# Rounding steps of the activation quantization: which engine runs them, in a two-layer kernel on eight cores

## The chip, the cores and the metric

The kernel runs on one Trainium2 chip, on all 8 of its cores. Each core computes one of the 8 sequences of the batch; the cores exchange nothing. The time is the device time in microseconds of the slowest core. A core has TensorE (PE, matrix products into eight PSUM banks), VectorE (DVE), ScalarE (ACT), GpSimd (POOL), SyncE (SP) and 16 DMA engines. The engines run their own instruction streams in the order in which they were written and meet at semaphores only.

## The reference

Input x is [8, 2048, 1024]. Two layers, each attention then feed-forward, and after each of the four the residual sum is layer-normalized:

- layer 0 attention is a time-mixed linear recurrence (four 1024x1024 products), layer 0 feed-forward has a gated pair of 1024 to 4096 products, two 4096x4096 products and one back to 1024;
- layer 1 attention is gated linear attention with 4 heads. Each of its products (q, k, v, g, gk1, gk2, o) takes a quantized input;
- layer 1 feed-forward is 1024 to 4096, a depthwise convolution over 3 tokens, silu, 4096 to 1024, both products with quantized inputs.

The quantization, which is all that the change touches, is

```
def act_quant(x):
    scale = 127.0 / jnp.clip(jnp.max(jnp.abs(x), axis=-1, keepdims=True), 1e-05)
    return jnp.clip(jnp.round(x * scale), -128.0, 127.0) / scale
```

with one scale for each token (the last axis is the features).

## The kernel before

The residual stream stays in SBUF as `XA`, feature-major. `Prog` records the instructions of each engine in the order in which the stage functions emit them; nothing reorders them. `P.op(engine, fn, after=[...])` appends one instruction and returns a token; `after` lists the tokens waited for. `vt` carries the last VectorE token through a stage, `stt` the last ScalarE token.

**Rounding.** `_round_fix` (L1398) rounds 128x1024 values in `Zb`: a cast to int32 into `Ib` (L1399), a cast back to bf16 into `Tb` (L1400), the difference `Zb - Tb` into `Db` (L1401), and two compare-and-add steps (L1404, L1406) which correct the cast whichever way it rounds. Every caller passes `en = "v"`, so all of it runs on VectorE; the branch for another engine is never taken.

**Its four callers**, and how often each calls it:

- `stage_l1attn`, projections: 8 blocks of 256 tokens, 5 projections (q, k, v, g, gk1, in this order), 2 groups of 128 tokens (`tt`): 80 calls. A call begins with the product with the norm weights (L991), the maximum (L995), four small steps (L998 to L1006), and the scaling by a column (L1010); after the rounding come the rescaling (L1013), eight transposes on TensorE (L1023) and two copies into `XQF` (L1029). After both groups the projection's matmuls follow (L1067 for q and k, L1086 for v and g, L1044 for gk1). The results leave PSUM on VectorE for q, k, v and gk1, and for g on ScalarE with silu (L1101): eight of those a block.
- `stage_l1attn`, the output product: per block 2 chunks of 128 tokens and 2 halves: 32 calls, with a scaling L1331 ahead and L1334 behind.
- `stage_l1ffn`, input: 4 quarters of 512 tokens, 4 groups: 16 calls, with L1540 ahead and L1543 behind.
- `_act_quant_fm` (L1421), the 4096 hidden features of a quarter: 16 pieces of 1024 columns in each of 4 quarters: 64 calls. Each is preceded by a product of two tensors (L1427) and followed by L1432 and L1434. The product waits for the end of the piece before it (`ch = vt`).

The weights of the projections come through one buffer `WL`, filled by POOL's queue; the norm weights through one buffer `NB`.

Of the kernel before, what the change touches and what calls it, by code (L numbers as in the profile page):

```python
# [10 lines left out]
AF = mybir.ActivationFunctionType  # L11
ALU = mybir.AluOpType
# [871 lines left out]
def stage_l1attn(ctx, toks):  # L884
# [6 lines left out]
    with ExitStack() as st_:  # L891
# [48 lines left out]
        vt = vz2  # L940
# [13 lines left out]
        for blk_i in range(8):  # L954
# [27 lines left out]
            for pi, (pnm, wnm, nnm, dout) in enumerate(NPROJ):  # L982
# [3 lines left out]
                for tt in range(2):  # L986
                    en = "v"
                    Zb, Ib, Tb, Db = (QSz, QSi, QSt, QSd) if tt == 0 else (Q2z, Q2i, Q2t, Q2d)
                    CLx = CL if tt == 0 else CL2
                    ch = vt  # L990
                    p1 = P.op(en, lambda v, tt=tt, Zb=Zb: v.tensor_mul(  # L991
                        Zb[:], X2[:, tt, :], NB[:, 0:1024]),
                        after=[d_nb, x2tok, ch, zb_free[tt]])
                    nb_free2[tt] = p1
                    p2 = P.op("v", lambda v, Zb=Zb, CLx=CLx: v.reduce_max(  # L995
                        CLx[:, 4:5], Zb[:], axis=AXX, apply_absolute_value=True),
                        after=[p1, vt])
# [12 lines left out]
                    q1 = P.op(en, lambda v, Zb=Zb, CLx=CLx: v.tensor_single_scalar(  # L1010
                        Zb[:], Zb[:], CLx[:, 7:8], ALU.mult), after=[p6, ch])
                    q6 = _round_fix(P, en, Zb, Ib, Tb, Db, Zb, q1)
                    q7 = P.op(en, lambda v, Zb=Zb, Tb=Tb, CLx=CLx: v.tensor_scalar(  # L1013
                        Zb[:], Tb[:], 1.0, CLx[:, 8:9], ALU.subtract, ALU.mult),
                        after=[q6])
                    vt = q7
                    xtp = []
                    for c in range(NC):
                        bank = 5 + c // 4
                        cc = c % 4  # L1020
                        a = [q7, bank_free[bank]] if (c % 4 == 0) else []
                        xtp.append(P.op("t", lambda t, c=c, bank=bank, cc=cc, Zb=Zb:
                                        t.transpose(  # L1023
                            PSB[bank][:, cc * 128:(cc + 1) * 128],
                            Zb[:, c * 128:(c + 1) * 128], IDB[:]), after=a))
                    zb_free[tt] = xtp[-1]
                    for half in range(2):
                        bank = 5 + half
                        ev = P.op("v", lambda v, tt=tt, half=half, bank=bank: v.tensor_copy(  # L1029
                            XQF[:, half * 4:(half + 1) * 4, tt * 128:(tt + 1) * 128],  # L1030
                            PSB[bank][:, 0:512].rearrange("p (c n) -> p c n", c=4)),
                            after=[xtp[half * 4 + 3], vt])
                        vt = ev
                        bank_free[bank] = ev
                    qtoks.append(vt)
# [151 lines left out]
            for cn in range(2):  # L1187
# [135 lines left out]
                for half in range(2):  # L1323
# [4 lines left out]
                        Zb[:], OG[:, half * 1024:(half + 1) * 1024],  # L1328
                        NOB[:, half * 1024:(half + 1) * 1024]),
                        after=[ch, w7, zb_free[half]])  # L1330
                    y2 = P.op(en, lambda v, Zb=Zb: v.tensor_single_scalar(  # L1331
                        Zb[:], Zb[:], CL[:, 7:8], ALU.mult), after=[y1])
                    y7_ = _round_fix(P, en, Zb, Ib, Tb, Db, Zb, y2)
                    y8 = P.op(en, lambda v, Zb=Zb, Tb=Tb: v.tensor_scalar(  # L1334
                        Zb[:], Tb[:], 1.0, CL[:, 8:9], ALU.subtract, ALU.mult),
                        after=[y7_])
# [58 lines left out]

def _round_fix(P, en, Zb, Ib, Tb, Db, M, prev):  # L1398
# [4 lines left out]
    if en == "v":
        o4 = P.op(en, lambda v, Tb=Tb, Db=Db: v.scalar_tensor_tensor(  # L1404
            Tb[:], Db[:], 0.5, Tb[:], ALU.is_ge, ALU.add), after=[o3])
        o5 = P.op(en, lambda v, Tb=Tb, Db=Db: v.scalar_tensor_tensor(  # L1406
            Tb[:], Db[:], -0.5, Tb[:], ALU.is_gt, ALU.add), after=[o4])
    else:
        o4a = P.op(en, lambda v, Db=Db, M=M: v.tensor_single_scalar(
            M[:], Db[:], 0.5, ALU.is_ge), after=[o3])  # L1410
        o4 = P.op(en, lambda v, Tb=Tb, M=M: v.tensor_add(Tb[:], Tb[:], M[:]),
                  after=[o4a])
        o5a = P.op(en, lambda v, Db=Db, M=M: v.tensor_single_scalar(
            M[:], Db[:], -0.5, ALU.is_gt), after=[o4])
        o5 = P.op(en, lambda v, Tb=Tb, M=M: v.tensor_add(Tb[:], Tb[:], M[:]),
                  after=[o5a])
    return o5


def _act_quant_fm(P, flat, UB, WB, QSV, QSG, vt, gt, ready=None):  # L1420
    piece = 1024  # L1421
    for pc in range(16384 // piece):
        o0 = pc * piece
# [3 lines left out]
        q1 = P.op(en, lambda v, o0=o0: v.tensor_mul(  # L1427
            flat[:, o0:o0 + piece], flat[:, o0:o0 + piece], UB[:, 0:piece]),
            after=[ch, ready if pc < 2 else None])
        q6 = _round_fix(P, en, flat[:, o0:o0 + piece], QI[:, 0:piece],  # L1430
                        QT[:, 0:piece], QD[:, 0:piece], QM[:, 0:piece], q1)
        q7 = P.op(en, lambda v, QT=QT: v.tensor_scalar(  # L1432
            QT[:, 0:piece], QT[:, 0:piece], 1.0, None, ALU.subtract), after=[q6])
        q8 = P.op(en, lambda v, o0=o0, QT=QT: v.tensor_mul(  # L1434
            flat[:, o0:o0 + piece], QT[:, 0:piece], WB[:, 0:piece]), after=[q7])
        vt = q8
    return vt, gt


def stage_l1ffn(ctx, toks):  # L1440
# [5 lines left out]
    with ExitStack() as st_:  # L1446
# [51 lines left out]
        for q in range(4):  # L1498
# [7 lines left out]
            for tt in range(4):  # L1506
# [5 lines left out]
                for c in range(NC):  # L1512
# [121 lines left out]
            for which, COLS, ROW in ((0, MX[:, 0:4], UR), (1, MX[:, 4:8], WR)):  # L1634
                for tt in range(4):
# [180 lines left out]
```

How the kernel before makes its waits and increments, by code:

```python
            def body(eng):  # L145
                seen = {}
                for i, rec in enumerate(prog.ops[e]):
                    for kind, val in rec["waits"]:
                        if seen.get(kind, 0) >= val:
                            continue
                        eng.wait_ge(prog.sems[kind], val)
                        seen[kind] = val
                    inst = rec["fn"](eng)
                    if rec["dma"] is not None:
                        inst.then_inc(prog.sems[rec["dma"]], 16)
                    amt = incs[e].get(i)
                    if amt:
                        inst.then_inc(prog.sems[e], amt)
```

## Time and profile before

| | |
|---|---|
| median of 3 runs | 12169.72 us (12141.12 to 12209.28) |
| the profiled execution's own time | 12209.73 us |
| its span on the slowest core (core 3), first to last instruction | 12208.2 us |
| spans of the eight cores | 12118.2 to 12208.2 us |
| mean granted TensorE clock, cores 0 to 3 and 4 to 7 | 0.697 and 0.704 |
| layer 1 attention, from the span's start | 6360 to 9880 us |
| layer 1 feed-forward | 10034 to 12110 us |

The profile is of one execution, on its slowest core. "Busy" counts an engine's instructions, not its waits, and a share over the whole span mixes eight stages with different limits; so the two stages that quantize are to be read by themselves. In a timeline a row gives the start, the duration, the engine, the line and the operation, and in brackets how long the engine had been idle and what released it. The granted clock is a share of 2.4 GHz; 0.5 is the lower of TensorE's two levels, 1.2 GHz.

### The profile page before, as it was taken

The page shows a single profiled execution, that of the slowest core. Times are in us where ns is not written, and L with a number is a line of the kernel's source. Part 1 is how long each engine was busy: PE and PEld are TensorE (multiplying, and loading weights), DVE is VectorE, ACT ScalarE, POOL GpSimd, SP SyncE. Part 2 cuts the span into 40 slices and gives each one's busy share as a digit, 9 for nine tenths or more (in the row PEclk, how much of TensorE's full clock was granted, in tenths as well). Part 3 has the DMA queues.
Part 4 walks back from the last instruction along what each step waited for, and adds up shares of the span by engine and source line. Part 5 has one row for each costly group of instructions (what it writes and reads, how often), then busy time and mean ns, then how long its engine had stood idle before and what let it go on. Part 6 is the DMA issues. An engine that isn't in the chain of part 4 may idle for free.

```text
span 12208.2 us, 72294 instructions; the slowest of 8 cores (12118.2 to 12208.2 us)
## 1 busy us (share of the span) xinstructions
PE 5413.1 (44%) x22678; PEld 2575.2 (21%) x22678; DVE 3719.3 (30%) x6428; ACT 1286.9 (11%) x2046; POOL 780.4 (6%) x1515
## 2 busy tenths in 40 slices
PE   3430016666666666666643333333333332413323
PEld 1120002222222222222221222222122221101112
DVE  6762231000000100000024444444444435353553
ACT  1232100000000100000021001001001021001011
POOL 0000450000000000000000000000000000000000
PEclk7765557888878787878766666666666666756666
DMA  4224432222222222222211111111111101101012
GB/s 114 76 73 125 139 92 40 43 42 45 45 38 43 39 43 42 42 42 43 41 29 52 60 44 43 60 52 40 55 60 43 54 14 30 55 11 45 25 30 78
DMA packets 171208, 637.27 MB, mean 52 GB/s; under 512 B 30976, under 2 KB 31360, under 8 KB 159568
## 3 DMA queue, kind: packets, MB, share of 16 engines
q0 software_dynamic: 125696, 480.99, 16.2%
q1 hardware_dynamic: 45136, 151.67, 4.2%
q8 instruction: 187, 3.06, 0.1%
q14 instruction: 189, 1.55, 0.0%
HBM read 794.50 MB, written 42.01 MB: 69 GB/s over the span
## 4 chain that ended last, share of the span: by engine, by line
PE 40%; DVE 27%; DMA 19%; issue 8%; ACT 4%; DVEq 1%; POOL 1%; ACTq 0%; SPq 0%; POOLq 0%
PE ps L824 17%; PE ps L776 5%; DMA f_wj<-h1R 4%; DMA f_wj<-h2R 4%; PE ps L1672 2%; PE ps L861 2%; DMA f_wj<-w1R 2%; PE ps L1086 2%; PE ps L1253 2%; PE ps L1571 1%; PE ps L1371 1%; DMA pre_in<-f1T 1%; DMA pre_in<-f2T 1%; PE ps L1067 1%; DMA b_wj<-q_f2T 1%
## 5 line engine op out<-in xcount | busy, mean ns | idle before, releaser
L824 PE MATMUL ps<-f_h,f_wj 128*128 128x512 bf16 x8192 | 2080.1, 422 | 1106.0 <-DMA f_wj<-h1R 554.8
L824 PEld LDWEIGHTS ps<-f_h,f_wj 128*128 128x128 bf16 x8192 | 868.6, 106 | 2317.5 <-issue 1648.6
L872 DVE SCALAR_TENSOR_TENSOR XA<-ps,SVEC,XA 128x512 f32<-128x512 f32 x32 | 24.0, 751 | 3547.3 <-PE ps L861 3544.9
L776 PE MATMUL ps<-f_h,f_wj 128*128 128x512 bf16 x2048 | 576.9, 452 | 527.5 <-DMA f_wj<-w1R 520.6
L1672 PE MATMUL ps<-b_hc,b_wj 128*128 128x512 bf16 x1024 | 281.3, 443 | 611.7 <-DVE b_hc L1434 469.3
L835 ACT ACTIVATE f_h<-ps,f_sc 128x512 bf16<-128x512 f32 x256 | 176.5, 689 | 2960.6 <-PE ps L824 2948.4
L776 PEld LDWEIGHTS ps<-f_h,f_wj 128*128 128x128 bf16 x2048 | 229.7, 112 | 874.3 <-issue 720.3
L1086 PE MATMUL ps<-a_wl,a_xqf 128*128 128x512 bf16 x1024 | 305.2, 471 | 150.7 <-DMA a_wl<-q_gwT 68.8
L796 DVE SCALAR_TENSOR_TENSOR f_h<-ps,f_sc,f_g 128x512 bf16<-128x512 f32 x128 | 96.1, 751 | 781.9 <-ACT f_g L786 775.2
L861 PE MATMUL ps<-f_h,f_wj 128*128 128x512 bf16 x1024 | 251.4, 411 | 137.3 <-DMA f_wj<-w3R 137.3
L1233 PE MATMUL ps<-a_qg,a_kp 128*128 128x128 f32 x256 | 76.4, 454 | 523.5 <-DVE a_kg L1226 523.5
L1616 PE MATMUL ps<-c_idb,b_hc 128*128 128x128 bf16 x512 | 74.9, 302 | 524.0 <-ACT b_hc L1599 397.6
L1672 PEld LDWEIGHTS ps<-b_hc,b_wj 128*128 128x128 bf16 x1024 | 111.1, 111 | 786.3 <-issue 705.0
L536 PE MATMUL ps<-l_xk,l_wk 128*128 128x512 bf16 x256 | 105.6, 587 | 351.9 <-DVE l_xr L522 190.3
L408 PE MATMUL ps<-pre_acc,c_ones 128*128 128x1 f32 x18 | 4.5, 319 | 570.0 <-POOL pre_acc L401 570.0
L1571 PE MATMUL ps<-b_xq,b_wj 128*128 128x512 bf16 x1024 | 238.9, 387 | 19.5 <-DMA b_wj<-q_f1T 11.7
L1371 PE MATMUL ps<-a_oqf,a_wl 128*128 128x128 bf16 x2048 | 177.1, 270 | 146.8 <-DMA a_wl<-q_owT 133.2
L694 PE MATMUL ps<-c_idf,ln_tm 128*128 128x128 f32 x384 | 93.2, 424 | 310.0 <-DVE ln_tm L675 310.0
L1023 PE MATMUL ps<-c_idb,a_q2z 128*128 128x128 bf16 x320 | 40.4, 306 | 417.5 <-DVE a_q2z L1013 417.5
L431 DVE TENSOR_SCALAR pre_in<-pre_in,pre_rs 128x1024 f32<-128x1024 f32 (+1 forms) x137 | 100.2, 732 | 395.4 <-DMA pre_in<-f1T 129.5
L1575 ACT ACTIVATE b_h<-ps,SCL 128x512 bf16<-128x512 f32 x128 | 88.3, 690 | 1248.0 <-PE ps L1571 1248.0
L1253 PE MATMUL ps<-a_S,a_qg 128*128 128x512 f32 x256 | 218.3, 1004 | 0.0
(338 smaller groups left out, 7677.3 us busy)
## 6 DMA issues: line engine op xcount, KB each, us to landing
f_wj<-h1R POOLq DMA_DIRECT2D x128, 512.0 KB, 5.9
f_wj<-h2R POOLq DMA_DIRECT2D x128, 512.0 KB, 5.7
a_wl<-q_owT POOLq DMA_DIRECT2D x32, 2048.0 KB, 7.7
b_wj<-q_f2T POOLq DMA_DIRECT2D x80, 512.0 KB, 4.7
pre_in<-f1T SPq DMA_DIRECT2D x64, 512.0 KB, 4.1
pre_in<-f2T SPq DMA_DIRECT2D x64, 512.0 KB, 3.9
a_wl<-q_vwT POOLq DMA_DIRECT2D x16, 2048.0 KB, 7.6
a_wl<-q_gwT POOLq DMA_DIRECT2D x16, 2048.0 KB, 7.6
```

What stands on the lines that cost most here:

```text
L431: v1 = P.op("v", lambda v: v.tensor_single_scalar(buf[0:rr, 0:cc], buf[0:rr, 0:cc], pre["rs"][0:rr, :], ALU.mult), after=[ld, state["v"]])
L536: mmK = P.op("t", lambda t, c=c, i=i, bk=bk: t.matmul(PS[bk][:, :], WK[:, i, c * 128:(c + 1) * 128], XK[:, i, :], start=(i == 0), stop=(i ...
L776: t.matmul(PS[bank][:, :], wb[:, i, :], XB[:, i, s2 * 512:(s2 + 1) * 512], start=(i == 0), stop=(i == NC - 1)),
L824: off=off, SRC=SRC: t.matmul(PS[bank][:, :], wb[:, i2, :], SRC[:, i * 1024 + off:i * 1024 + off + 512], start=(i == 0), stop=(i == 31)),
L835: DST=DST: s.activation(DST[:, j * 1024 + off:j * 1024 + off + 512], PS[bank][:, :], AF.Gelu, scale=SC[:, scoff + j:scoff + j + 1]),
L861: off=off: t.matmul(PS[bank][:, :], wb[:, i2, :], H0[:, i * 1024 + off:i * 1024 + off + 512], start=(i == 0), stop=(i == 31)),
L1067: mm = P.op("t", lambda t, i=i, j=j, bank=bank: t.matmul(PS[bank][:, 0:256], WLv[:, i, j * 128:(j + 1) * 128], XQF[:, i, :], start=(i == 0 ...
L1086: t.matmul(PS[bank][:, :], XQF[:, i, tt * 128:(tt + 1) * 128], WLv[:, i, ds * 512:(ds + 1) * 512], start=(i == 0), stop=(i == NC - 1)),
L1253: omm = P.op("t", lambda t, h=h, j=j: t.matmul(PS[3][:, :], QG[:, j, :], S[:, 2 * h + j, :], start=(j == 0), stop=False), after=[f3, bank_ ...
L1371: cc=cc: t.matmul(PS[bank][:, cc * 128:(cc + 1) * 128], WLv[:, i, jj * 128:(jj + 1) * 128], OQF[:, rnd * 8 + i, :], start=(rnd == 0 and i ...
L1571: mm = P.op("t", lambda t, slot=slot, i=i, j=j, bank=bank: t.matmul(PS[bank][:, :], FWJ[slot][:, i, :], XQ3[:, i, :], start=(i == 0), stop ...
L1672: t.matmul(PS[bank][:, :], FWJ[s_][:, i2, :], HC[:, i, :], start=(i == 0), stop=(i == 31)),
```

## The change

The two casts of `_round_fix` are now ScalarE activations with the function Identity. The difference and the two corrections stay on VectorE. In three of the four callers the scaling just ahead of the rounding goes to ScalarE too, as an Identity with a column as its scale; in `_act_quant_fm` the product ahead of it stays on VectorE. The ScalarE token is threaded through (`stt`). The unused branch and the argument's effect are gone.

```
@@ stage_l1attn, projections (stage_l1attn output and stage_l1ffn input alike)
-                    q1 = P.op(en, lambda v, Zb=Zb, CLx=CLx: v.tensor_single_scalar(
-                        Zb[:], Zb[:], CLx[:, 7:8], ALU.mult), after=[p6, ch])
-                    q6 = _round_fix(P, en, Zb, Ib, Tb, Db, Zb, q1)
+                    q1 = P.op("s", lambda s, Zb=Zb, CLx=CLx: s.activation(
+                        Zb[:], Zb[:], AF.Identity, scale=CLx[:, 7:8]),
+                        after=[p6, ch, stt])
+                    stt = q1
+                    q6, s6 = _round_fix(P, en, Zb, Ib, Tb, Db, Zb, q1, stt)
+                    stt = s6
...
@@ _round_fix
-    o1 = P.op(en, lambda v, Zb=Zb, Ib=Ib: v.tensor_copy(Ib[:], Zb[:]), after=[prev])
-    o2 = P.op(en, lambda v, Ib=Ib, Tb=Tb: v.tensor_copy(Tb[:], Ib[:]), after=[o1])
-    o3 = P.op(en, lambda v, Zb=Zb, Tb=Tb, Db=Db: v.tensor_sub(Db[:], Zb[:], Tb[:]),
-              after=[o2])
...
+    o1 = P.op("s", lambda s, Zb=Zb, Ib=Ib: s.activation(Ib[:], Zb[:], AF.Identity),
+              after=[prev, sprev])
+    o2 = P.op("s", lambda s, Ib=Ib, Tb=Tb: s.activation(Tb[:], Ib[:], AF.Identity),
+              after=[o1])
+    o3 = P.op("v", lambda v, Zb=Zb, Tb=Tb, Db=Db: v.tensor_sub(Db[:], Zb[:], Tb[:]),
+              after=[o2, prev])
...
+    return o5, o2
@@ _act_quant_fm
-        q6 = _round_fix(P, en, flat[:, o0:o0 + piece], QI[:, 0:piece],
-                        QT[:, 0:piece], QD[:, 0:piece], QM[:, 0:piece], q1)
+        q6, s6 = _round_fix(P, en, flat[:, o0:o0 + piece], QI[:, 0:piece],
+                            QT[:, 0:piece], QD[:, 0:piece], QM[:, 0:piece], q1, st[0])
+        st[0] = s6
```

On VectorE, the quantization of the first group for gk1 in the first block stands in a row like this before (`a_q...` are the quantization's buffers, `a_cl` its columns, `a_xqf` the transposed result, `a_x` the input in token-major form):

```order
L998 TENSOR_SCALAR a_cl<-a_cl 128x1
L1001 RECIPROCAL a_cl<-a_cl 128x1
L1003 SCALAR_TENSOR_TENSOR a_cl<-a_cl 128x1
L1006 TENSOR_SCALAR a_cl<-a_cl 128x1
L1010 TENSOR_SCALAR a_qz<-a_qz,a_cl 128x1024
L1399 CAST a_qi<-a_qz 128x1024
L1400 CAST a_qt<-a_qi 128x1024
L1401 TENSOR_TENSOR a_qd<-a_qz,a_qt 128x1024
L1404 SCALAR_TENSOR_TENSOR a_qt<-a_qd,a_qt 128x1024
```

Of the changed kernel the same place reads, the difference's line being L1409 now:

```order
L998 TENSOR_SCALAR a_cl<-a_cl 128x1
L1001 RECIPROCAL a_cl<-a_cl 128x1
L1003 SCALAR_TENSOR_TENSOR a_cl<-a_cl 128x1
L1006 TENSOR_SCALAR a_cl<-a_cl 128x1
L1409 TENSOR_TENSOR a_qd<-a_qz,a_qt 128x1024
L1411 SCALAR_TENSOR_TENSOR a_qt<-a_qd,a_qt 128x1024
L1413 SCALAR_TENSOR_TENSOR a_qt<-a_qd,a_qt 128x1024
```

Three instructions of 128x1024 are gone from VectorE's row, and nothing has come in between: L1006 is followed by the difference that needs their result.

On ScalarE, in the first block of the attention, the row before is this (`a_sg` is the gate, `a_wf` and `a_g1t` belong to the decay; x8 are the eight silu of g):

```order
L978 ACTIVATE a_cl<-a_cl 128x2
L1101 ACTIVATE a_sg<-ps,SCL 128x512 x8
L1109 ACTIVATE a_wf,a_cl<-a_g1t 128x16
L1118 ACTIVATE a_cl<-a_cl 128x1
L1109 ACTIVATE a_wf,a_cl<-a_g1t 128x16
```

In the changed kernel it is this, from the second group's quantization for g on (L1104 is the silu's line there, L1112 the decay's):

```order
L1010 ACTIVATE a_q2z<-a_q2z,a_cl 128x1024
L1405 ACTIVATE a_q2i<-a_q2z 128x1024
L1407 ACTIVATE a_q2t<-a_q2i 128x1024
L1104 ACTIVATE a_sg<-ps,SCL 128x512 x8
L1010 ACTIVATE a_qz<-a_qz,a_cl 128x1024
L1405 ACTIVATE a_qi<-a_qz 128x1024
L1407 ACTIVATE a_qt<-a_qi 128x1024
L1010 ACTIVATE a_q2z<-a_q2z,a_cl 128x1024
L1405 ACTIVATE a_q2i<-a_q2z 128x1024
L1407 ACTIVATE a_q2t<-a_q2i 128x1024
L1112 ACTIVATE a_wf,a_cl<-a_g1t 128x16
```

The three steps of gk1's first group now stand behind all eight silu of g on the same engine. In all, VectorE has 512 instructions fewer and ScalarE 512 more (3 x 128 + 2 x 64); the rows of POOL and SP are the same as before.

## Rows read from the trace of the kernel before

**Rows 1.** Section 1 of the page: busy us, share of span, instructions.
```profile
PE 5413.1 (44%) x22678; PEld 2575.2 (21%) x22678; DVE 3719.3 (30%) x6428; ACT 1286.9 (11%) x2046; POOL 780.4 (6%) x1515
```

**Rows 2.** Attention and feed-forward stretch: length, busy PE, PEld, DVE, ACT, POOL, then clock.
```profile
6360.00:9880.00 3520.00, 1300.28 (x6360) 766.78 (x6360) 1640.86 (x3155) 323.78 (x548) 66.01 (x124) 0.64 0.15 51
10034.00:12110.00 2076.00, 678.28 (x3134) 303.20 (x3132) 959.61 (x1542) 183.47 (x261) 110.60 (x208) 0.64 0.12 37
```

**Rows 3.** Section 4 of the page: the chain that ended last, by engine.
```profile
PE 40%; DVE 27%; DMA 19%; issue 8%; ACT 4%; DVEq 1%; POOL 1%; ACTq 0%; SPq 0%; POOLq 0%
```

**Rows 4.** Timeline, quantization before the k projection: start, us, engine, line, operation.
```profile
6855.23 0.15 DVE L1006 TENSOR_SCALAR a_cl<-a_cl 128x1 f32<-128x1 f32 x1
6855.49 0.49 DVE L1010 TENSOR_SCALAR a_q2z<-a_q2z,a_cl 128x1024 bf16<-128x1024 bf16 x1
6856.08 0.69 DVE L1399 CAST a_q2i<-a_q2z 128x1024 int32<-128x1024 bf16 x1
6856.88 0.69 DVE L1400 CAST a_q2t<-a_q2i 128x1024 bf16<-128x1024 int32 x1
6857.68 0.69 DVE L1401 TENSOR_TENSOR a_q2d<-a_q2z,a_q2t 128x1024 bf16<-128x1024 bf16 x1
...
6861.77 1.01 PE L1023 MATMUL ps<-c_idb,a_q2z 128*128 128x128 bf16 x8 [10.32 <-DVE a_q2z L1013]
```

**Rows 5.** Groups of ScalarE instructions, shapes apart: busy us, mean ns, idle before.
```profile
L1101 ACT ACTIVATE a_sg<-ps,SCL 128x512 bf16<-128x512 f32 x64 | 44.1, 689 | 143.3 <-PE ps L1086 143.2
...
L1204 ACT ACTIVATE a_et<-a_gt 128x256 f32<-128x256 f32 x64 | 26.8, 418 | 6.2 <-ACT a_qg L1201 0.4
...
L560 ACT ACTIVATE l_sr<-ps 128x512 bf16<-128x512 f32 x32 | 19.1, 598 | 0.4
...
L1282 ACT ACTIVATE a_wf<-a_og 128x1024 f32<-128x1024 bf16 x16 | 16.9, 1058 | 156.1 <-DVE a_og L1274 156.1
...
L672 ACT ACT_TABLE_LOAD x3 | 3.8, 1283 | 4.4 <-DVE ln_cols L670 4.4
```

**Rows 6.** Timeline: hand-overs between VectorE and ScalarE, and on ScalarE alone.
```profile
7018.75 1.91 ACT L1181 ACTIVATE a_wf<-a_wf 128x2048 f32<-128x2048 f32 x1 [0.37 <-ACT a_wf L1179]
...
7029.92 0.48 DVE L1218 TENSOR_SCALAR a_et<-a_gt 128x128 f32<-128x128 f32 x2
7030.55 0.42 ACT L1222 ACTIVATE a_et<-a_et 128x256 f32<-128x256 f32 x1 [1.73 <-DVE a_et L1218]
7031.07 0.43 DVE L1226 TENSOR_TENSOR a_kg<-a_et,a_k 128x256 f32<-128x256 f32 x1 [0.67 <-ACT a_et L1222]
...
7079.46 1.06 ACT L1282 ACTIVATE a_wf<-a_og 128x1024 f32<-128x1024 bf16 x1 [9.13 <-DVE a_og L1274]
7080.43 0.19 ACT L1282 ACTIVATION_READ_ACCUMULATOR a_wf<-a_og 128x1 f32 x1
```

**Rows 7.** Timeline, quantization before gk1, first 128 tokens: blocks 1, 2 and 8.
```profile
6536.83 0.69 DVE L1401 TENSOR_TENSOR a_qd<-a_qz,a_qt 128x1024 bf16<-128x1024 bf16 x1
...
6539.60 0.69 ACT L1101 ACTIVATE a_sg<-ps,SCL 128x512 bf16<-128x512 f32 x1 [1.04 <-PE ps L1086]
...
6973.57 0.69 DVE L1401 TENSOR_TENSOR a_qd<-a_qz,a_qt 128x1024 bf16<-128x1024 bf16 x1
...
6976.42 0.69 ACT L1101 ACTIVATE a_sg<-ps,SCL 128x512 bf16<-128x512 f32 x1 [1.04 <-PE ps L1086]
...
6977.03 0.59 DVE L1013 TENSOR_SCALAR a_qz<-a_qt,a_cl 128x1024 bf16<-128x1024 bf16 x1
...
9609.39 0.69 DVE L1401 TENSOR_TENSOR a_qd<-a_qz,a_qt 128x1024 bf16<-128x1024 bf16 x1
...
9611.88 0.69 ACT L1101 ACTIVATE a_sg<-ps,SCL 128x512 bf16<-128x512 f32 x1 [1.04 <-PE ps L1086]
```

**Rows 8.** Timeline, one piece of the feature-major quantization.
```profile
10319.58 0.69 DVE L1427 TENSOR_TENSOR b_hc<-b_hc,b_ub 128x1024 bf16<-128x1024 bf16 x1
...
10321.97 0.69 DVE L1401 TENSOR_TENSOR b_qd<-b_hc,b_qt 128x1024 bf16<-128x1024 bf16 x1
```

More of the change, by code:

```diff
@@ L1330, in stage_l1attn @@
                         after=[ch, w7, zb_free[half]])
-                    y2 = P.op(en, lambda v, Zb=Zb: v.tensor_single_scalar(
-                        Zb[:], Zb[:], CL[:, 7:8], ALU.mult), after=[y1])
-                    y7_ = _round_fix(P, en, Zb, Ib, Tb, Db, Zb, y2)
+                    y2 = P.op("s", lambda s, Zb=Zb: s.activation(
+                        Zb[:], Zb[:], AF.Identity, scale=CL[:, 7:8]),
+                        after=[y1, stt])
+                    stt = y2
+                    y7_, sy = _round_fix(P, en, Zb, Ib, Tb, Db, Zb, y2, stt)
+                    stt = sy
                     y8 = P.op(en, lambda v, Zb=Zb, Tb=Tb: v.tensor_scalar(
@@ L1394, in stage_l1attn, with _round_fix, _act_quant_fm @@
         return dict(v=P.tok("v"), t=P.tok("t"), s=P.tok("s"))
-def _round_fix(P, en, Zb, Ib, Tb, Db, M, prev):
-    o1 = P.op(en, lambda v, Zb=Zb, Ib=Ib: v.tensor_copy(Ib[:], Zb[:]), after=[prev])
-    o2 = P.op(en, lambda v, Ib=Ib, Tb=Tb: v.tensor_copy(Tb[:], Ib[:]), after=[o1])
-    o3 = P.op(en, lambda v, Zb=Zb, Tb=Tb, Db=Db: v.tensor_sub(Db[:], Zb[:], Tb[:]),
-              after=[o2])
[L1403 to L1420, printed above, removed]
+def _round_fix(P, en, Zb, Ib, Tb, Db, M, prev, sprev=None):
+    o1 = P.op("s", lambda s, Zb=Zb, Ib=Ib: s.activation(Ib[:], Zb[:], AF.Identity),
[4 more added lines that the diff above has]
+              after=[o2, prev])
+    o4 = P.op("v", lambda v, Tb=Tb, Db=Db: v.scalar_tensor_tensor(
+        Tb[:], Db[:], 0.5, Tb[:], ALU.is_ge, ALU.add), after=[o3])
+    o5 = P.op("v", lambda v, Tb=Tb, Db=Db: v.scalar_tensor_tensor(
+        Tb[:], Db[:], -0.5, Tb[:], ALU.is_gt, ALU.add), after=[o4])
+    return o5, o2
+def _act_quant_fm(P, flat, UB, WB, QSV, QSG, vt, gt, ready=None, stt=None):
+    st = [stt]
     piece = 1024
@@ L1436, in _act_quant_fm @@
         vt = q8
-    return vt, gt
+    return vt, gt, st[0]
 def stage_l1ffn(ctx, toks):
@@ L1539, in stage_l1ffn @@
                 vt = a5
-                b1 = P.op(en, lambda v, Zb=Zb, CLx=CLx: v.tensor_single_scalar(
-                    Zb[:], Zb[:], CLx[:, 3:4], ALU.mult), after=[a5, ch])
-                b6 = _round_fix(P, en, Zb, Ib, Tb, Db, MSKF[tt % 2], b1)
+                b1 = P.op("s", lambda s, Zb=Zb, CLx=CLx: s.activation(
+                    Zb[:], Zb[:], AF.Identity, scale=CLx[:, 3:4]),
+                    after=[a5, ch, stt])
+                stt = b1
+                b6, sb6 = _round_fix(P, en, Zb, Ib, Tb, Db, MSKF[tt % 2], b1, stt)
+                stt = sb6
                 b7 = P.op(en, lambda v, Zb=Zb, Tb=Tb, CLx=CLx: v.tensor_scalar(
@@ L1654, in stage_l1ffn @@
                 bank_free[6] = bev
-            vt, gt = _act_quant_fm(P, HC[:, :, :].rearrange("p c n -> p (c n)"),
-                                   UB, WB, (QI, QT, QD, MSKF[0]),
-                                   (Q2i, Q2t, Q2d, MSKF[1]), vt, gt, ready=vt)
+            vt, gt, stt = _act_quant_fm(P, HC[:, :, :].rearrange("p c n -> p (c n)"),
+                                        UB, WB, (QI, QT, QD, MSKF[0]),
+                                        (Q2i, Q2t, Q2d, MSKF[1]), vt, gt,
+                                        ready=vt, stt=stt)
             hq_tok = (vt, gt)
```

## The prediction

> **What bounds the kernel now.** I read the page's busy shares first, then the busy time of the two stages that quantize, the chain of waits, and last the timeline of single calls. The shares [rows 1] show no full engine: TensorE 44%, VectorE 30%, ScalarE 11%. The two stages alone [rows 2] say more: in the attention's 3520 us VectorE is busy for 1641 (47%) and ScalarE for 324 (9%), in the feed-forward's 2076 us it is 960 (46%) and 183 (9%). ScalarE looks like free room. But a share can't say whether an engine is waited for. The chain [rows 3] gives VectorE 27% of the span, nearly its whole busy share. The timeline shows why [rows 4]: from the last column step (L1006) to the difference (L1401) VectorE runs L1010, L1399 and L1400 with gaps of 0.1 us, and TensorE's transposes end an idle of 10.32 us on this chain. One call is one string of dependent steps; nobody else works meanwhile. So what counts is not VectorE's load but how long the string is from L1006's end to L1401's start.
>
> **What the string costs now.** L1006 ends at 6855.38 and L1401 starts at 6857.68 [rows 4]: 2.30 us for 0.49 + 0.69 + 0.69 and four gaps. In the feature-major pieces only the two casts lie in it: L1427 ends at 10320.27, L1401 starts at 10321.97 [rows 8]: 1.70 us.
>
> **What it costs on ScalarE.** No row of before shows an activation from bf16 to int32 or back.
>
> - An activation of 128x1024 from bf16 takes 1058 ns (L1282), which I take for each cast [rows 5]. Underneath I bound it by VectorE's own 0.69 [rows 4].
> - The scaling has a column as its scale. At 128x512 from PSUM one with a scale column (L1101) takes 689 ns and one without (L560) 598 [rows 5], so a column costs 91; 1058 + 91 = 1149 ns.
> - VectorE to ScalarE: L1218 ends at 7030.40, L1222 starts at 7030.55, 0.15 us. Back: L1222 ends at 7030.97, L1226 starts at 7031.07, 0.10 us [rows 6].
> - ScalarE waiting for itself: L1204's 64 starts behind L1201 cost 6.2 us of idle, 0.10 each [rows 5]. One such start took 0.37 [rows 6]; that is my upper bound.
>
> The string becomes 0.15 + 1.149 + 0.10 + 1.058 + 0.10 + 1.058 + 0.10 = 3.71 us in place of 2.30, +1.41. In a feature-major piece it is 0.15 + 1.058 + 0.10 + 1.058 + 0.10 = 2.46 in place of 1.70, +0.76.
>
> At this place the Trainium skill (page "ScalarE: Activation LUTs", section "What ACT_TABLE_LOAD costs") gives 186 ns + 0.833 ns for each element and about 93 ns for each column operand, 1039 and 1132 ns here, near my rows; but it also says that back-to-back activations overlap by about 93 ns. What that would make is rival C.
>
> **Does anything hide it?** VectorE executes in the written order, and there the difference follows L1006 directly; the instructions after it need it. So VectorE idles through the three activations. TensorE waits for the transposes' input as before. The weight load beside it is hidden already (the transposes and then the matmuls follow VectorE), so a longer string hides no more of it.
>
> **Where it is worse.** In ScalarE's row, gk1's first group stands behind the eight silu of g. Before, this group's VectorE string ran under g's last matmuls: in block 2 the difference started at 6973.57 and the rescaling ended at 6977.62, while the last silu only ended at 6977.11 [rows 7]. Now the scaling waits for that silu: 6977.11 + 0.10 + 1.149 + 0.10 + 1.058 + 0.10 + 1.058 + 0.10 = 6980.77 is the difference's new start, +7.20 us. Block 1 gives 6540.29 + 3.66 - 6536.83 = +7.12, block 8 gives 9612.57 + 3.66 - 9609.39 = +6.85 [rows 7]; over 8 blocks about 7.1 each. Every other call finds ScalarE idle: v's results leave on VectorE, and in the feed-forward the evictions are over.
>
> **The sum.** Of the 80 projection calls 72 are of the plain kind, with 32 of the output product and 16 of the feed-forward's input: 120 x 1.41 = 169 us. The feature-major pieces: 64 x 0.76 = 49 us. gk1's first groups: 8 x 7.1 = 57 us. Together +275 us. Of these some 57 + 72 x 1.41 + 32 x 1.41 = 204 fall in the attention and 71 in the feed-forward.
>
> Table loads cost nothing: an Identity stands in each token group of the layer norms (64 groups) between functions of other tables, and only 3 loads stand ahead of L672's square root [rows 5]. The layer-0 stages aren't touched. TensorE's granted clock of 0.64 in both stages [rows 2] is half way between the levels; the pauses ahead of its bursts are already 10 us and become 12, so I count nothing for it, within some 20 us of either sign.
>
> The rows come from an execution of 12209.7 us (span 12208.2 and 1.5 around it), 0.3% above the median of the runs shown. On it the sum gives 12485; on the median, 12169.7 + 275 = 12445 us. That is the predicted time.
>
> **Rivals.**
>
> A. VectorE's load is the limit, and the move relieves it. VectorE loses 128 x (0.49 + 0.10) + 384 x (0.69 + 0.11) = 383 us of string. If ScalarE's steps lay wholly beside other VectorE work, the kernel would come out at 12170 - 383 = 11787. It is decided between L1006 and the difference: VectorE would need independent work there, and from 1.41 us of it in each call the kernel would break even. For it speaks the 47% share; against it the written order, where nothing stands there. The skill's page "Perfetto Trace Analysis", section "Optimizing Scalar/DVE Operations", says that the move may make sense where VectorE is saturated, which 47% isn't, and that a step with a fast mode is quicker on VectorE: the scaling (L1010) takes 0.49 us there [rows 4] where a cast of the same width takes 0.69. That rule speaks against this change, above all against moving the scaling.
>
> B. ScalarE's steps are dearer. If each activation behind another started 0.37 after it and not 0.10 [rows 6], the 128 x 2 + 64 = 320 such starts add 86 us: 12531.
>
> C. Activations behind one another overlap. L1282's accumulator read starts at 7080.43, 0.09 before the activation's end at 7080.52 [rows 6]. If the 320 starts did so, 0.19 each would go, 61 us: 12384. Against it: that pair has no semaphore wait, and L1204, which has one as the new steps do, starts 0.10 after the end. [...]
>
> D. The casts are cheaper than an activation to fp32 at this width. At VectorE's 0.69 us for each of the 384, 384 x 0.36 = 138 us go: 12307. Nothing speaks for it but that no row shows an int32 activation.
>
> E. gk1's first group isn't held up, because ScalarE reaches it earlier than I think. Then it costs 1.41 and not 7.1: 8 x 5.7 = 46 less, 12399. The order of the row speaks against it.
>
> **How the numbers follow.** The forecast gets 0.80, B 0.06, C 0.04, D 0.03, E 0.04, and A 0.03. All but A end over 1% above the median. What a measurement of this kernel can tell from no change is about 0.5%, 61 us. A in full would be faster; in part it could end within 0.5%. So faster 0.02, the same 0.02, slower 0.96. The range goes from 12350, which takes in C's and E's times with the 30 us by which the runs shown differ from their median, to 12555, which takes in B's with most of that; D and A stay outside.
>
> **What would show it.** In the changed kernel's profile: 512 fewer VectorE instructions, its busy time down by 128 x 0.49 + 384 x 0.69 = 328 us to about 3390; ScalarE's up by 128 x 1.149 + 384 x 1.058 = 553 us to about 1840. Every difference waits on ScalarE, 3.7 us each after L1006 and 2.46 in a feature-major piece: some 3.6 x 128 + 2.4 x 64 = 614 us of VectorE idle with ScalarE as the releaser. The first difference of gk1 starts some 3.7 us after the last silu's end in all eight blocks. The attention grows from 3520 to about 3724 us, the feed-forward from 2076 to about 2147, and the rest stays. The prediction is wrong if VectorE runs something between L1006 and the difference, if an activation to or from int32 differs from 1.06 us, or if the stages before 6205 us move.

## The result

The changed kernel takes 12516.94 us (median of 10 runs, 12481.18 to 12624.57), the kernel before, run beside it, 12203.15 (10 runs). The ratio of the two is 1.0282, 95% interval 1.0253 to 1.0311: 2.8% slower, 310 to 380 us, where the prediction said 275. The profiled execution took 12481.2 us, its slowest core (now core 5) spans 12479.6.

In some executions the cores of a die, or all cores, show a lower granted clock and take longer, and in many of the experiments that makes whole times scatter by over 1%. Two measures are steadier and are used below: the stages' lengths as medians over the eight cores of a profiled execution, and the span of the fastest core in each run, as a median over all runs of a kernel ("fastest core"). Where cores are called undisturbed, their clock in layer 0's feed-forward was 0.82 or more. The stages run from the first cast of layer 0's feed-forward (L757) to the attention's memset of `STAT` (L939), from there to the feed-forward's memset of `b_one` (so with the layer norm between), and from there to the last matmul on `b_one`.

| us | layer 0 feed-forward | layer 1 attention | layer 1 feed-forward |
|---|---|---|---|
| before | 4552 | 3670 | 2026 |
| changed | 4595 | 3875 | 2106 |
| difference | +43 | +205 | +80 |
| predicted | 0 | +204 | +71 |

The rest (layer 0 attention, last layer norm) is the same within 5 us.

Section 1 of the page of the changed kernel (busy us, share, instructions), to set beside [rows 1], and the chain's shares by engine, beside [rows 3]:

```profile
PE 5355.4 (43%) x22678; PEld 2572.8 (21%) x22678; DVE 3388.5 (27%) x5916; ACT 1836.3 (15%) x2558; POOL 780.0 (6%) x1515
```

```profile
PE 39%; DVE 24%; DMA 19%; ACT 9%; issue 7%; DVEq 1%; POOL 1%; ACTq 0%; SPq 0%; POOLq 0%
```

VectorE's busy time fell from 3719 to 3388 us (3390 was predicted), ScalarE's rose from 1287 to 1836 (1840). The chain shows what that did: VectorE's share went from 27 to 24%, ScalarE's from 4 to 9%. The load left one engine of the chain for another engine of the chain. By stage, with the columns of [rows 2] (length, busy PE, PEld, DVE, ACT, POOL, clock):

```profile
6336.00:10058.00 3722.00, 1293.37 (x6352) 771.50 (x6352) 1427.51 (x2823) 688.06 (x884) 62.47 (x119) 0.64 0.14 48
10212.00:12330.00 2118.00, 685.02 (x2866) 299.75 (x2866) 837.08 (x1350) 369.17 (x434) 103.77 (x195) 0.63 0.11 33
```

VectorE is busy for 38% of the attention and 40% of the feed-forward now, and both stages are longer.

The groups of ScalarE, shapes apart, answer what no row of before could:

```profile
L1407 ACT ACTIVATE a_qt<-a_qi 128x1024 bf16<-128x1024 int32 x56 | 59.2, 1056 | 5.1
...
L1405 ACT ACTIVATE a_qi<-a_qz 128x1024 int32<-128x1024 bf16 x56 | 59.1, 1056 | 5.2
...
L1010 ACT ACTIVATE a_qz<-a_qz,a_cl 128x1024 bf16<-128x1024 bf16 x40 | 45.9, 1147 | 635.6 <-DVE a_cl L1006 634.8
```

The casts to and from int32 take 1056 ns (1058 was taken from [rows 5]) and the scaling 1147 (1149). The idle ahead of a cast, 5.1 us over 56, is the 0.1 us of [rows 5] again. On VectorE's side each difference (L1409) now waits on ScalarE:

```profile
L1409 DVE TENSOR_TENSOR a_qd<-a_qz,a_qt 128x1024 bf16<-128x1024 bf16 x56 | 38.8, 693 | 253.4 <-ACT a_qt L1407 253.4
...
L1409 DVE TENSOR_TENSOR b_q2d<-b_hc,b_q2t 128x1024 bf16<-128x1024 bf16 x32 | 22.2, 693 | 81.1 <-ACT b_q2t L1407 81.1
```

The six groups of this line wait 684 us in all, released by L1407; before, the difference (L1401) waited for no other engine. The prediction had said 614: its round 3.6 and 2.4 us leave out some 0.1 us a call, and it left out the 8 x 5.7 us by which gk1's first groups wait longer than the others. A timeline of gk1's first group in block 2, to set beside [rows 7]:

```profile
6977.90 0.15 DVE L1006 TENSOR_SCALAR a_cl<-a_cl 128x1 f32<-128x1 f32 x1
...
6983.03 0.69 ACT L1104 ACTIVATE a_sg<-ps,SCL 128x512 bf16<-128x512 f32 x1 [1.04 <-PE ps L1089]
...
6983.81 1.15 ACT L1010 ACTIVATE a_qz<-a_qz,a_cl 128x1024 bf16<-128x1024 bf16 x1
6985.05 1.06 ACT L1405 ACTIVATE a_qi<-a_qz 128x1024 int32<-128x1024 bf16 x1
6986.20 1.06 ACT L1407 ACTIVATE a_qt<-a_qi 128x1024 bf16<-128x1024 int32 x1
6987.36 0.69 DVE L1409 TENSOR_TENSOR a_qd<-a_qz,a_qt 128x1024 bf16<-128x1024 bf16 x1 [9.30 <-ACT a_qt L1407]
```

The columns are ready at 6978.05, but ScalarE is at the silu of g until 6983.72. The scaling starts 0.09 after it, and the difference 3.64 us after the silu's end (3.66 predicted; 3.63 or 3.64 in all eight blocks). And a feature-major piece, beside [rows 8]:

```profile
10502.97 0.69 DVE L1428 TENSOR_TENSOR b_hc<-b_hc,b_ub 128x1024 bf16<-128x1024 bf16 x1
10504.08 1.06 ACT L1405 ACTIVATE b_qi<-b_hc 128x1024 int32<-128x1024 bf16 x1 [69.60 <-DVE b_hc L1428]
10505.23 1.06 ACT L1407 ACTIVATE b_qt<-b_qi 128x1024 bf16<-128x1024 int32 x1
10506.46 0.69 DVE L1409 TENSOR_TENSOR b_qd<-b_hc,b_qt 128x1024 bf16<-128x1024 bf16 x1 [2.80 <-ACT b_qt L1407]
```

The product ends at 10503.66 and the difference starts at 10506.46. This first piece takes 2.80 us; the median of the 64 is 2.52, of before 1.70.

### The profile page after: what moved, and what is told of

Read it like the earlier page. It is cut to its first block, busy times and chain, and to the rows that moved or that the text cites. A ratio compares the mean times of both kernels' runs of the same rounds, so it can differ in the third digit from the quotient of the medians.

```text
span 12479.6 us, 72546 instructions; the slowest of 8 cores (12432.7 to 12479.6 us)
## 1 busy us (share of the span) xinstructions
PE 5355.4 (43%) x22678; PEld 2572.8 (21%) x22678; DVE 3388.5 (27%) x5916; ACT 1836.3 (15%) x2558; POOL 780.0 (6%) x1515
## 4 chain that ended last, share of the span: by engine, by line
PE 39%; DVE 24%; DMA 19%; ACT 9%; issue 7%; DVEq 1%; POOL 1%; ACTq 0%; SPq 0%; POOLq 0%
PE ps L824 16%; PE ps L776 5%; DMA f_wj<-h1R 4%; DMA f_wj<-h2R 4%; PE ps L1089 2%; PE ps L1678 2%; PE ps L861 2%; DMA f_wj<-w1R 2%; PE ps L1256 2%; PE ps L1576 2%; PE ps L1377 2%; DMA pre_in<-f1T 1%; DMA pre_in<-f2T 1%; DMA b_wj<-q_f2T 1%; PE ps L1070 1%
## 5 line engine op out<-in xcount | busy, mean ns | idle before, releaser
L824 PE MATMUL ps<-f_h,f_wj 128*128 128x512 bf16 x8192 | 2029.1, 414 | 1125.4 <-DMA f_wj<-h1R 564.5
L824 PEld LDWEIGHTS ps<-f_h,f_wj 128*128 128x128 bf16 x8192 | 858.0, 105 | 2296.5 <-issue 1496.9
L776 PE MATMUL ps<-f_h,f_wj 128*128 128x512 bf16 x2048 | 573.5, 450 | 531.8 <-DMA f_wj<-w1R 524.8
L861 PE MATMUL ps<-f_h,f_wj 128*128 128x512 bf16 x1024 | 253.4, 414 | 140.5 <-DMA f_wj<-w3R 140.5
L1576 PE MATMUL ps<-b_xq,b_wj 128*128 128x512 bf16 x1024 | 251.5, 405 | 16.7 <-DMA b_wj<-q_f1T 11.6
L395 ACT ACTIVATE pre_in<-pre_in 128x1024 f32<-128x1024 f32 (+1 forms) x137 | 137.9, 1006 | 667.6 <-DMA pre_in<-f2T 258.1
L1026 PE MATMUL ps<-c_idb,a_qz 128*128 128x128 bf16 x320 | 40.4, 306 | 452.9 <-DVE a_qz L1016 452.9
```

The costliest lines, as they stand in the source:

```text
L395: s1 = P.op("s", lambda s: s.activation(buf[0:rr, 0:cc], buf[0:rr, 0:cc], AF.Abs, accum_out=red[0:rr, :]), after=[ld, state["s"], state["r ...
L776: t.matmul(PS[bank][:, :], wb[:, i, :], XB[:, i, s2 * 512:(s2 + 1) * 512], start=(i == 0), stop=(i == NC - 1)),
L824: off=off, SRC=SRC: t.matmul(PS[bank][:, :], wb[:, i2, :], SRC[:, i * 1024 + off:i * 1024 + off + 512], start=(i == 0), stop=(i == 31)),
L861: off=off: t.matmul(PS[bank][:, :], wb[:, i2, :], H0[:, i * 1024 + off:i * 1024 + off + 512], start=(i == 0), stop=(i == 31)),
L1576: mm = P.op("t", lambda t, slot=slot, i=i, j=j, bank=bank: t.matmul(PS[bank][:, :], FWJ[slot][:, i, :], XQ3[:, i, :], start=(i == 0), stop ...
```

## The experiments

Theory S: the change costs what its strings of dependent steps grow by, because nothing stands beside ScalarE's steps in VectorE's written order. Its rivals are named in the expectations. Two questions came up on the way: why layer 0's feed-forward, with the same code, grew too, and whether the same engine split pays once it is overlapped. The attention and feed-forward columns are the stages above.

### The kernel before again: e0_before_again

No edit.

> The kernel before, once more, for its stages. Theory S (the change costs what its strings cost, about 278 us, and what is above that lies in stages whose code is the same and varies from execution to execution): time within 0.3% of the kernel before; the stretch from the first cast of layer 0's feed-forward to the attention's memset lands anywhere between 4540 and 4620 us on the eight cores, as in the two profiles so far. Rival R (layer 0 really is 45 us longer in the changed kernel): all its undisturbed cores stay at 4540 to 4560 us.

Time 1.0033 of before (0.9986 to 1.0080). Attention 3669, feed-forward 2026 us. Layer 0's feed-forward: 4519 to 4543 us on six cores, 4668 and 4676 on cores 2 and 3, whose clock over the whole run was 0.689 and 0.688. So on undisturbed cores this kernel lies at 4519 to 4559 in two profiles, and the 4580 to 4602 of all eight cores of the changed kernel aren't in that scatter. This spoke against S as I had written it there.

### Only the casts: e1_casts_only

```
-                    q1 = P.op("s", lambda s, ...: s.activation(Zb[:], Zb[:], AF.Identity, scale=CLx[:, 7:8]), ...)
+                    q1 = P.op(en, lambda v, ...: v.tensor_single_scalar(Zb[:], Zb[:], CLx[:, 7:8], ALU.mult), ...)
```

and so at the two other scalings. (Against the changed kernel; `...` stands for arguments left out.)

> As the changed kernel, but the scaling ahead of the rounding (L1010, L1334, L1543) stays on VectorE; only the two casts are on ScalarE. Theory S: the string from the scaling's end grows by 0.8 us instead of 1.4 in 184 calls (147 us), and gk1's first group by 6 us in 8 blocks (48): 195 us more than before, 1.6%, about 80 us less than the change. Rival L (VectorE's load matters, so every step taken off it helps): this is slower than the change, over 2.8%.

Attention 3796 (+126; S gives 131), feed-forward 2091 (+65; 66): 191 us by stages against 195. The fastest core is at 12319, 101 us under the 12420 of the changed kernel on the same chip (e7_change_again). The whole-time ratio, 1.0199 (1.0092 to 1.0306), is too wide to tell alone. Taking more off VectorE made the kernel slower; rival L falls. Moving the scaling costs 0.6 us a call: VectorE took 0.49 us for it, and ScalarE takes 1.15.

### gk1 left on VectorE: e2_gk1_on_vector

```
+                    if pnm == "gk1":
+                        q1 = P.op(en, ... v.tensor_single_scalar(Zb[:], Zb[:], CLx[:, 7:8], ALU.mult), ...)
+                        q6 = _round_fix_v(P, Zb, Ib, Tb, Db, q1)
+                    else:
```

> As the changed kernel, but gk1's scaling and casts (16 of 192 calls) stay on VectorE. Theory S: gk1's first group no longer waits for the last silu of g, 57 + 11 us go, the attention stretch falls from 3875 to about 3807 us; the time is some 0.55% below the change's. Rival O (the place behind the silu is harmless, ScalarE catches up): only 16 x 1.4 = 22 us go, 0.2%.

Attention 3804 us, 71 under the change, where S says 68 and rival O 22. A twelfth of the calls carries over a third of the attention's loss, because ScalarE's row is in use there. In this profile most cores had a lower clock (0.682 to 0.691), and the attention's length differs from core to core (3793 to 3816), but not by the 46 us that part the two theories. The whole time (1.0222, 1.0103 to 1.0341) again tells less than the stage.

### Only the feature-major pieces: e3_pieces_only

The changed `_round_fix` is used by `_act_quant_fm` alone; the other three callers are as before.

> The kernel before, with the casts on ScalarE only in the 64 feature-major pieces. Theory S: 64 x 0.83 = 53 us more, 0.4%, all of it in layer 1's feed-forward, and the attention stretch stays at 3670 us. Rival R (something outside the strings is slower once the kernel uses ScalarE so): 100 us or more.

Feed-forward 2079 (+52; 53 expected), attention 3669 (unchanged), layer 0's feed-forward 4541. Time 1.0052 (0.9996 to 1.0109). S holds, and here nothing is added outside.

### Pieces overlapped: e4_pieces_overlapped

```
+    pend = front(0, vt, st)
+    for pc in range(n):
+        nxt = front(pc + 1, vt, st) if pc + 1 < n else None   # product on VectorE, casts on ScalarE
...
+        vt = back(pc, pend[0], pend[1], vt)                   # difference, corrections, rescaling
+        pend = nxt
```

(Shortened; the two functions and the handing on of the tokens are left out.)

> As the kernel with only the feature-major pieces' casts on ScalarE, but the product of piece n+1 is written ahead of the difference of piece n, so ScalarE casts n+1 while VectorE corrects n. Theory S (the move costs because nothing stands beside it): VectorE's piece falls from 7.20 to 5.61 us, 64 x 1.59 = 102 us less but for about 2.5 us at the first piece of each quarter; layer 1's feed-forward falls from 2026 to about 1930 us, the attention stays at 3670. Rival P (the engines slow each other when they work on the same tiles' partitions at once): VectorE's instructions lengthen and less than half of it is left, 1980 us or more.

Feed-forward 1932 us (1930 expected), attention 3669. The timeline of two pieces, VectorE and ScalarE:

```profile
10324.22 0.69 DVE L1454 TENSOR_TENSOR b_qd<-b_hc,b_qt 128x1024 bf16<-128x1024 bf16 x1
10324.27 1.06 ACT L1425 ACTIVATE b_q2i<-b_hc 128x1024 int32<-128x1024 bf16 x1 [3.38 <-DVE b_hc L1442]
...
10325.42 1.06 ACT L1425 ACTIVATE b_q2t<-b_q2i 128x1024 bf16<-128x1024 int32 x1
...
10329.80 0.69 DVE L1454 TENSOR_TENSOR b_q2d<-b_hc,b_q2t 128x1024 bf16<-128x1024 bf16 x1
```

The differences (L1454) are 5.58 us apart instead of 7.18, and VectorE doesn't wait: the casts of the next piece start at 10324.27 and end at 10326.48, under the corrections of this one. VectorE's 0.69 and 1.23 us are what they were, so rival P falls. Time 0.9889 (0.9827 to 0.9952). The same instructions on the same engines as in e3_pieces_only, 147 us apart by the stage: the order decides.

### Everything overlapped: e5_all_overlapped

```
                 for tt in range(2):
                     ... columns (L991 to L1006)
+                    o2 = _round_front(P, Zb, Ib, Tb, CLx[:, 7:8], p6, stt)   # scaling and casts, ScalarE
+                for tt in range(2):
+                    q6 = _round_back(P, Zb, Tb, Db, o2s[tt])                 # difference and corrections
...
+                        bank = (5, 3)[tt] + c // 4
```

(The projections only, shortened.)

> All four callers with scaling and casts on ScalarE, as in the change, but written in pairs: both groups' columns and ScalarE steps first, then both differences and corrections, then all four copies; the second group's transposes use banks 3 and 4. Pieces as in e4_pieces_overlapped. Theory S: 32 pairs of projections save 5.7 us, gk1's none, 16 pairs of the output product 3.4, 8 pairs of the feed-forward's input 5.7, the pieces 96: attention from 3670 to about 3434, feed-forward from 2026 to about 1884, in all 378 us less than before, 3.1%. Rival A' (VectorE isn't on the path after all, other waits come up at once): less than 150 us.

Ratio 0.9660 (0.9564 to 0.9757). Attention 3404, feed-forward 1869 us: 266 and 157 less than before, 423 together where 378 was expected. A pair of groups of the q to g projections, from the first product to the last copy, takes 16.7 us at the median and took 22.6 before: 5.9 less where 5.7 was expected. So most of the attention's surplus of 30 us isn't in these pairs; where it lies isn't shown. One projection pair:

```profile
6832.32 0.15 DVE L1006 TENSOR_SCALAR a_cl<-a_cl 128x1 f32<-128x1 f32 x1
6832.58 0.69 DVE L991 TENSOR_TENSOR a_q2z<-a_x,a_nb 128x1024 bf16<-128x1024 bf16 x1
6832.62 1.15 ACT L1425 ACTIVATE a_qz<-a_qz,a_cl 128x1024 bf16<-128x1024 bf16 x1 [37.51 <-DVE a_cl L1006]
...
6833.86 1.06 ACT L1419 ACTIVATE a_qi<-a_qz 128x1024 int32<-128x1024 bf16 x1
...
6835.01 1.06 ACT L1419 ACTIVATE a_qt<-a_qi 128x1024 bf16<-128x1024 int32 x1
...
6835.55 0.15 DVE L1006 TENSOR_SCALAR a_cl<-a_cl 128x1 f32<-128x1 f32 x1
6836.16 1.15 ACT L1425 ACTIVATE a_q2z<-a_q2z,a_cl 128x1024 bf16<-128x1024 bf16 x1
6836.17 0.69 DVE L1437 TENSOR_TENSOR a_qd<-a_qz,a_qt 128x1024 bf16<-128x1024 bf16 x1 [0.46 <-ACT a_qt L1419]
...
6840.03 0.69 DVE L1437 TENSOR_TENSOR a_q2d<-a_q2z,a_q2t 128x1024 bf16<-128x1024 bf16 x1
...
6844.07 2.01 DVE L1039 COPY a_xqf<-ps 128x512 bf16<-128x512 bf16 x4
```

The second group's product starts 0.11 us after the first group's columns end, while ScalarE works from 6832.62 on. VectorE waits 0.46 us for the first group's casts, and then runs without another wait to the four copies at 6844.07. From the first columns' end (6832.47) to there it takes 11.60 us. Layer 0's feed-forward is 4590 us, close to the changed kernel's 4595.

### The order by itself: e6_reordered_on_vector

```
-CE = "s"
+CE = "v"
```

> The same order and banks as e5_all_overlapped, but scaling and casts on VectorE. It separates what the order gives by itself from what ScalarE gives. Theory S: only the waits for the transposes go, 1.8 us a pair: attention from 3670 to about 3569, feed-forward from 2026 to about 2012, 115 us less than before, 0.9%. Rival Q (the order alone does it): as fast as e5_all_overlapped, within 50 us.

Ratio 0.9887 (0.9740 to 1.0033). Attention 3608, feed-forward 2003: 62 and 24 less than before, 86 together. The clock was 0.681 to 0.692 in this profile (layer 0's feed-forward at 4662 to 4738), so its stages are the weaker of the two measures. The fastest core is 110 us under the kernel before beside it (12004 against 12113), and that of e5_all_overlapped 386 (11727). So the order alone gives 86 to 110 us, near the 115 expected, and the larger part comes from ScalarE working beside VectorE: 337 us by the stages, and 276 or more by the fastest cores, where e5_all_overlapped also bears the longer layer 0. Rival Q falls.

### The change again: e7_change_again

> The changed kernel once more, for its stages. Theory S: attention 3875 and feed-forward 2106 us again (within 10), while layer 0's feed-forward lands anywhere from 4530 to 4700 us. Rival R (the changed kernel is slower in layer 0): 4580 to 4600 on all cores again.

Attention 3877, feed-forward 2102; the fastest core is at 12420 against 12113 of the kernel before beside it, +307. Layer 0's feed-forward is 4584 to 4588 us on cores 0 to 3 and, at a clock of 0.685, 4699 to 4706 on cores 4 to 7. The extra 45 us or so of layer 0 belong to the kernel: R holds there.

### A longer stream of ScalarE: e8_before_long_scalar

```
+            for k in range(64):
+                stt = P.op("s", lambda s: s.activation(CL2[:, 14:15], STAT[:, 62:63], AF.Identity), after=[stt])
```

> The kernel before with 512 more ScalarE activations of one column (64 in each block of the attention, where ScalarE waits for over 100 us; they read a constant and write a spare column). ScalarE's stream is then as long as the changed kernel's, VectorE's as before. Open is why layer 0's feed-forward, with the same code, lasts 4584 to 4602 us on undisturbed cores in the changed kernel and in e5, 4519 to 4559 before. Theory T (the length of ScalarE's stream decides, through where things come to lie or how they are fetched): 4580 to 4600. Rival U (VectorE's shorter stream does it, or the executions' scatter): 4520 to 4560. Attention 3670 and feed-forward 2026 us in any case.

The clock was only 0.687 to 0.691 in the profile, and layer 0's feed-forward lasted 4615 to 4678, so no core lies in either range as it was written. But cores of equal clock can be set side by side (clock of this stage alone, lengths of its cores in us):

| clock in layer 0's feed-forward | before, e0_before_again | longer ScalarE stream | the change, e7_change_again |
|---|---|---|---|
| 0.79 | 4668, 4676 | 4655 to 4678 | 4699 to 4706 |
| 0.80 | 4617, 4624 | 4615, 4617 | none |
| 0.82 to 0.83 | 4519 to 4559 | none | 4580 to 4602 |

At the same clock the longer ScalarE stream costs nothing that shows, and the change costs some 30 to 50 us. Ratio 0.9987 (0.9931 to 1.0043). The fastest core is 27 us over before in the medians (12131 against 12104), but its two lowest values are the same (12096 and 12097 against 12092 and 12099). Theory T falls.

### The change with VectorE's old length: e9_change_long_vector

```
+                if pnm == "gk1":
+                    for k in range(64):
+                        vt = P.op("v", lambda v: v.memset(CL2[:, 15:16], 0.0), after=[vt])
```

> The changed kernel with 512 more VectorE memsets of one column (64 in each block, ahead of gk1's first group, where VectorE waits 19 us for its norm weights; they take about 10 us). VectorE's stream is then as long as before, ScalarE's as in the change. Rival U (VectorE's shorter stream): layer 0's feed-forward falls back to 4520 to 4560 us. Theory T: it stays at 4580 to 4600. Attention 3875 and feed-forward 2106 us in any case.

Layer 0's feed-forward is 4523 to 4548 us on all eight cores, attention 3877, feed-forward 2102. Start and end of layer 0's feed-forward (L757's first, L939) on core 4, of the changed kernel:

```profile
L757 DVE CAST f_h<-XA x16: 674/684/694, 1732.9 to 3955.9; 128x1024 bf16<-128x1024 f32 x16
...
L939 DVE MEMSET STAT<- x1: 59/59/59, 6330.2 to 6330.2; 128x1 f32 x1
```

of e9_change_long_vector:

```profile
L757 DVE CAST f_h<-XA x16: 675/687/697, 1729.5 to 3923.3; 128x1024 bf16<-128x1024 f32 x16
...
L939 DVE MEMSET STAT<- x1: 59/59/59, 6258.6 to 6258.6; 128x1 f32 x1
```

6330.2 - 1732.9 = 4597.3 us against 6258.6 - 1729.5 = 4529.1, with not one instruction of that stage changed. Where the time goes shows on the stage's largest group of matmuls, L824, on core 4 (busy us, mean ns, idle before), of the kernel before

```profile
L824 PE MATMUL ps<-f_h,f_wj 128*128 128x512 bf16 x8192 | 2004.5, 410 | 1102.9 <-DMA f_wj<-h1R 553.7 <-DMA f_wj<-h2R 549.3
```

and of the changed one:

```profile
L824 PE MATMUL ps<-f_h,f_wj 128*128 128x512 bf16 x8192 | 2032.3, 414 | 1124.2 <-DMA f_wj<-h2R 562.2 <-DMA f_wj<-h1R 562.0
```

28 us more of busy time and 21 more of waiting for weights. The waiting isn't one event: the stage has 128 such waits, and their median is 8.76 us instead of 8.56.

Ratio 1.0192 (1.0118 to 1.0265). The fastest core is at 12380, against 12104 of before beside it: +276 us, where the changed kernel without the memsets is 307 over (e7_change_again). 512 instructions more made the changed kernel faster.

### Both together: e10_overlapped_long_vector

The same memsets, 72 in each block, in e5_all_overlapped; VectorE then has 64 instructions more than before (6492).

> e5_all_overlapped with 576 more VectorE memsets of one column (72 in each block, ahead of gk1's first group, where VectorE waits for its norm weights), so that VectorE's stream is again as long as before. Theory U (a shorter VectorE stream is what makes layer 0's feed-forward longer by some 45 us, as e9_change_long_vector points to): layer 0's feed-forward falls from 4590 to 4520 to 4560, attention 3404 and feed-forward 1869 us stay, the undisturbed cores come to about 11690, some 430 us under the kernel before. Rival (e9's fall was chance): 4580 to 4600 as in e5, 11735.

Ratio 0.9626 (0.9588 to 0.9665), 11741.64 us against 12166.38: the fastest version here. The fastest core is at 11664.6 to 11667.5 in its six runs, against 11719.7 to 11820.9 in the seven of e5_all_overlapped: 61 us at the medians. It is 446 us under the kernel before beside it (12112); of this the order alone gave 110 (e6_reordered_on_vector), so some 336 us come from ScalarE's part. Layer 0's feed-forward is 4509 to 4522 on cores 0, 1, 6 and 7, 4555 and 4557 on 4 and 5, and 4656 and 4650 on 2 and 3 with the lowest clocks (0.703 and 0.706); attention 3400, feed-forward 1869.

### VectorE's stream longer than before: e11_before_longer_vector

The same 64 memsets in each block, in the kernel before.

> The kernel before with 512 more VectorE memsets in the same place, so a VectorE stream longer than before. If only a shorter stream hurts, layer 0's feed-forward is 4520 to 4560 us on undisturbed cores; if any departure from the old length does, 4570 or more; if a longer one helps, under 4510. Attention 3670 us, feed-forward 2026.

Ratio 1.0012 (0.9980 to 1.0043), layer 0's feed-forward 4520 to 4553, attention 3669. A stream longer than before neither hurts nor helps.

## Why the prediction was right, and by how much not

- **What bounds it.** Right. VectorE's 47% in the attention was no queue of work but one string, and e5_all_overlapped shows the other side: with VectorE work placed beside ScalarE's, the same split is 3.4% faster than before.
- **ScalarE's prices.** Right to 2 ns each, and the hand-overs too: the median string from L1006's end to the difference is 3.70 us (3.71), 2.29 before. In the pieces it is 2.52, not 2.46: 4 us over the 64.
- **Where it is worse.** Right: the 80 projection calls have 343 us between L1006's end and the difference, where before they had 185; 158 us more, as 72 x 1.41 + 57 predicts. e2_gk1_on_vector left both of gk1's groups on VectorE and got 71 back (68 by the same sum).
- **The sum.** The strings grow by some 278 us against 275 (158 in the projections, 45 in the output product, 23 in the feed-forward's input, 52 in the pieces), and the fastest core of e9_change_long_vector, in which layer 0 isn't longer, is 276 over before.
- **The time.** 12517 us were measured where 12445 were predicted, 72 more. 33 of these are the kernel before, which took 12203 beside the change and not 12170. Against that the change costs 314 us by the medians and 344 by the ratio; the sum of the strings and layer 0's 43 us give 318. The range held, with 38 us to its upper end.
- **The step that failed** is "The layer-0 stages aren't touched". Their code isn't, but layer 0's feed-forward was 43 us longer in the medians (4552 to 4595). That is enough for the gap between the 275 predicted and the 307 by which the fastest core lies over before (e7_change_again). A sum over strings can't see it. The prediction did name it as a sign that would prove it wrong.
- **The clock.** Its term was put at nothing, and the clock of the two stages was 0.64 and 0.63 after 0.64 and 0.64. But 0.64 isn't half way between the levels 0.5 and 1, as the prediction has it; it lies nearer to the lower one. No number rests on that.
- **The rivals.** A's mechanism is real and its condition was the written order; its break-even point was passed only when the order was changed. B, C and D fall by the rows of the changed kernel: a start behind another activation takes 0.1 us, without overlap and without the 0.37, and a cast takes the full 1056 ns. The Trainium skill's overlap of back-to-back activations (page "ScalarE: Activation LUTs", section "What ACT_TABLE_LOAD costs") doesn't come about here, where the second waits for the first by a semaphore: the 5.1 us of idle ahead of 56 casts show it. Where the second doesn't need the first, the trace of before has it: in 14 places an activation of L395 starts 0.10 us before the end of one of L560 or L701, as at 368.27 against 368.38 us. E falls by the eight 3.64.
- **Table loads.** None was added: the slowest core has 120 in both kernels.

**What stays open** is why a shorter VectorE stream lengthens a stage ahead of it, and whether its length is the cause at all. With 128 VectorE instructions fewer, layer 0's feed-forward is 4541 and 4534 us as a median over eight cores (e3, e4), with 384 fewer 4561 (e1), and with 512 fewer 4595 and 4590 (the change, e5). Padding VectorE back to its length or a little over removed it twice. But it doesn't grow with the number missing: with 464 fewer (e2_gk1_on_vector) the two cores at a clock of 0.82 are at 4560 and 4564 us, against 4541 to 4559 on the six cores of before at that clock and 4580 to 4602 in the change. So a length that works little by little isn't the cause: the extra time shows clearly only in the versions with all 512 gone. Whether the place of the instructions in memory, their fetch, or the cores' relative timing on the weight loads is behind it, no run here tells; all the memsets stood in one place.

## What to carry to other kernels

A half-idle engine is no reason to give it work: ask what the giver will do meanwhile. If the next instruction in its written order needs the result, the move costs the difference of the two durations and both hand-overs, in every call; write the next tile's independent part in between first, and the same move can pay, as it did here. Look, too, for what is already queued on the engine that takes the work: here eight evictions made 8 calls of 192 carry a fifth of the loss.

## What was not expected of the hardware

Layer 0's feed-forward depends on code that runs thousands of microseconds later. In the change, with 512 fewer VectorE instructions, its median is 43 us longer than before and 60 longer than in e9_change_long_vector (4580 to 4602 on the eight cores against 4523 to 4548), where 512 one-column memsets in a place where VectorE waits anyway give it back. So a difference under 0.5% between two versions of this kernel isn't evidence on the edit until the stages without the edit have been compared as well.
